# A pack's products ahead of the rest of its vector work, sums in two PSUM banks, one gate per pack for the gathers

## The chip, the core and the metric

The kernel runs on one core of a Trainium2 chip. The metric is the device time of one execution in microseconds (us). Engines are called by their names in the profile: PE (TensorE; PEld is its weight load), DVE (VectorE), ACT (ScalarE), POOL (GpSimd) and SP (SyncE, which only issues transfers here).

## The reference, cut to what matters

A graph of 12,500 nodes with 32 features and 400,000 edges, sorted by their target `dst`. Two layers, each in pre-norm form:

```python
h = jnp.maximum(_layernorm(x, axis=-1), 0.0)
x = x + _L0_gnn_ref(h, Wq, Wk, Wv, Wo, edge_index)      # attention over a node's edges
h = jnp.maximum(_layernorm(x, axis=-1), 0.0)
x = x + _L1_gnn_ref(h, edge_weight, edge_attr_3, edge_index, w1, b1, w2, b2)
```

The second layer is the tensor product, and the change lies in it:

```python
R = relu(abs_distances[:, None] @ w1 + b1) @ w2 + b2      # 384 radial weights an edge
Y = spherical_harmonics(rel_vec)
Fj = features[src]                                         # a gathered row of 32 an edge
# for each pair of blocks (lo, li) and each lf:
acc = acc + _NORM[i] * einsum('euv,ef,evi,ofi->euo', Rb[..., k], Yf, Fb, C)
out = zeros.at[dst].add(msg)                               # summed over a node's edges
```

## The kernel before

The program has five stages: a prologue (layer norm, projections), the attention over the edges (`attention`, its gathers at L534), the node update, the tensor product over the edges (`tensor_product`), and the node sums. In both edge stages the edges lie in 128 partitions by 3132 slots, and POOL gathers the source's row for each slot by one indirect DMA of 128 rows: 3132 of them for `kv` in the attention and 3132 for `feat` in the tensor product (L988).

The tensor product works in 58 chunks of 54 slots. A chunk is three packs of 18 slots, so there are 174 packs, and a turn of the loops has six (`TURN`). A pack is cut in six groups of three slots (`TRI`), called g0 to g5 here, and in two halves (`s` = 0 and 1) of three groups. For a pack:

- SP (`stack_up`) loads the hidden layer of the pack, transposed, into one of two slots of `stack` and `capped`.
- PE's `radial` multiplies it by `whigh` and `wlow`, six matmuls a group (L1003, L1004), into one of two places of `psR`. It runs two groups ahead of DVE: the place of group g is free when DVE's product of group g-2 is done.
- DVE's `products(i, j, s)` multiplies `psR` by the operands `ops`, three instructions a group (L1221), into `prod`. `fold` (L1230) adds a few of the 16 planes of `prod` in place.
- PE's `sums` adds the planes of `prod` for a half by matmuls against the identity into `psS` (L1014 for the planes that need no fold, L1017 for the folded ones). `psS` is one bank. ACT's `evict` (L1063) copies it to `red`.
- DVE's `rotate_back` (L1236), `add_back` (L1247, L1249, L1250) and `scan` (L1260) turn the previous pack's sums back, add them and scan them along the slots; ACT's `seeds` writes a part of `seed` and the flags `same_c` between, and `store` copies `run` out and issues its transfer.
- DVE's `rotate` (L1185) and `operands` (L1194) make the next pack's operands from the gathered `feat`; ACT's `scalars` and `turned` copy parts of `ops`.

The order is written out by hand on each engine. On DVE a pack goes: products of half 0, `rotate_back` of the pack before, `fold`, `add_back`, a signal `half_done`, products of half 1, `scan`, `fold`, `rotate` and `operands` of the next pack. On PE each half has its three radial groups (two ahead) and then its sums. POOL's 18 gathers of a pack go to one of three `feat` buffers, with two gates: the first nine wait for `feat_free` (raised in `operands`), the other nine for `half_done`. Both are primed with three.

```python
order = [j for j in range(FOLDS[s], JC) if not JC // 2 <= j < JC // 2 + FOLDS[s]]
```

`FOLDS` is 3 for half 0 and 2 for half 1, so the sums are 10 + 3 and 12 + 2 matmuls; the profile records two entries for each of these fp32 matmuls. `same_c` lies in PSUM, in the bank `psF`.

Of the kernel before, what the change touches and what calls it, by code (L numbers as in the profile page):

```python
# [31 lines left out]
ALU = mybir.AluOpType  # L32
ACT = mybir.ActivationFunctionType
AX = mybir.AxisListType

P = 128
# [15 lines left out]
GROUPS = 3  # L52
# [825 lines left out]
def tensor_product(nc, a, k):  # L878
# [11 lines left out]
    with ExitStack() as ctx:  # L890
# [23 lines left out]
        psR = pb("psR", [P, 2, TRI, 512])  # L914
        psS = pb("psS", [P, 512])
        psF = pb("psF", [P, 512])
        same_c = psF[:, 0:VU * P1].rearrange("p (c t) -> p c t", t=P1)

# [3 lines left out]
        feat_here = [sem(f"feat_here{h}") for h in range(PACKS)]  # L922
        feat_free, frame_free, stored = sem("feat_free"), sem("frame_free4"), sem("stored4")
# [4 lines left out]
        seeded, vec_done, chunk_begun, half_done = sem("seeded"), sem("vec_done4"), sem("chunk_begun4"), sem("half_done")  # L928

        with nc.Block(no_gpsimd_drain=True) as block:  # L930
# [44 lines left out]
            @block.gpsimd  # L975
            def _(pool):
                own_block(pool)
                with pool.Fori(0, PAIRS) as i:
                    for b in range(2):
                        pool.wait_ge(src_loaded[b], i * 16 + 16)  # L980
                        for h in range(PACKS):
                            pool.wait_ge(feat_free, i * TURN + b * PACKS + h + 1)
                            pool.sem_inc(chunk_begun, 1)
                            for t in range(PACK):
                                if t == MIDWAY:
                                    pool.wait_ge(half_done, i * TURN + b * PACKS + h + 1)
                                    pool.sem_inc(chunk_begun, 1)
                                nc.gpsimd.indirect_dma_start(  # L988
                                    feat[h][:, t, :], None, a["h2"],
                                    bass.IndirectOffsetOnAxis(ap=src_i[b][:, h * PACK + t:h * PACK + t + 1].bitcast(U32), axis=0)).then_inc(feat_here[h], 16)  # L990

            @block.tensor
            def _(pe):
                def radial(i, g):


                    pack, slot = g // GPP, g // GPP % 2
                    if g % GPP == 0:
                        pe.wait_ge(stacked[slot], (i + pack // 2) * 32 + 32)
                    pe.wait_ge(prod_done, 3 * (i * (2 * GPP) + g) + 3)  # L1000
                    for t in range(TRI):
                        at = ((g % GPP) * TRI + t) * P
                        nc.tensor.matmul(psR[:, g % 2, t, 0:384], stack[:, slot, at:at + P], whigh[:, :], start=True, stop=False)  # L1003
                        last_mm = nc.tensor.matmul(psR[:, g % 2, t, 0:384], capped[:, slot, at:at + P], wlow[:, :], start=False, stop=True)  # L1004
                    last_mm.then_inc(radial_ready, 1)

                def sums(i, s):

                    r, q = s % 2, i * (2 * SPP) + s
                    pe.wait_ge(sum_free, q + 2)  # L1010
                    pe.wait_ge(prod_done, q * (3 * GROUPS) + 3 * GROUPS + 6)
                    order = [j for j in range(FOLDS[s], JC) if not JC // 2 <= j < JC // 2 + FOLDS[s]]
                    for n, j in enumerate(order):
                        nc.tensor.matmul(psS[:, 0:GC].rearrange("p (t c) -> p t c", c=COLS), ident[:, :], prod[r][:, :, j, :], start=(n == 0), stop=False)  # L1014
                    pe.wait_ge(prod_ready, q + 1)
                    for j in range(FOLDS[s]):
                        last_mm = nc.tensor.matmul(psS[:, 0:GC].rearrange("p (t c) -> p t c", c=COLS), ident[:, :], prod[r][:, :, j, :], start=False, stop=(j == FOLDS[s] - 1))  # L1017
                    last_mm.then_inc(sum_ready, 1)


                pe.wait_ge(scales_steps, 1)
                nc.tensor.matmul(psS[0:1, 0:P], tops[:, :], ident[:, :], start=True, stop=True).then_inc(scales_back, 1)
                pe.wait_ge(scales_steps, 2)
                nc.tensor.matmul(psS[:, 0:3], ones_row[:, :], scales0[:, 1:4], start=True, stop=True).then_inc(scales_back, 1)
                pe.wait_ge(scales_steps, 3)
                radial(0, 0)
                radial(0, 1)

                def body(i, last):
                    for s in range(2 * SPP):  # L1030
                        for g in range(GROUPS * s + 2, GROUPS * s + GROUPS + 2):
                            if not last or g < 2 * GPP:
                                radial(i, g)
                        sums(i, s)
                for i in range(TWO_PACKS):
                    body(i, i == TWO_PACKS - 1)

            @block.scalar
            def _(act):
# [18 lines left out]
                def evict(i, j, s):  # L1058

                    if s == 0:  # L1060
                        act.wait_ge(red_free, i * TURN + j + 1)
                    act.wait_ge(sum_ready, i * (TURN * SPP) + j * SPP + s + 1)
                    nc.scalar.activation(red[j % 2][:, s * NINE:(s + 1) * NINE, :].rearrange("p t c -> p (t c)"),  # L1063
                                         psS[:, 0:GC], ACT.Copy, scale=scales[:, 2:3]).then_inc(sum_free, 1)

# [22 lines left out]
                def body(i, first, last):  # L1088
                    for j in range(TURN):
                        begun, more = not (first and j == 0), not (last and j == TURN - 1)  # L1090
                        if begun:
                            evict(i, j - 1, SPP - 1)
                            seeds(i, j - 1)
                        if not (first and j < 2):
                            store(i, j - 2)
                        for s in range(SPP - 1):
                            evict(i, j, s)
                        if more:
# [6 lines left out]
                pairs_apart(act, body)  # L1105
                evict(PAIRS - 1, TURN - 1, SPP - 1)
                seeds(PAIRS - 1, TURN - 1)
# [5 lines left out]
            def _(vec):  # L1113
                v = nc.vector
                for primed, n in ((feat_free, PACKS), (half_done, PACKS), (prod_done, 6), (sum_free, 2), (ops_free, 2),
                                  (red_free, 2), (scanned, 1), (run_copied, 1)):
                    vec.sem_inc(primed, n)
# [5 lines left out]
                step(v.memset(run[:, :, PACK:P1], 0.0))  # L1123
                step(v.memset(same_c, 0.0))
                vec.sem_inc(rows_set, 1)
# [23 lines left out]
                at0 = lambda n: tops0[:, n:n + 1]  # L1149
                step(v.tensor_reduce(at0(3), psS[0:1, 0:HID], axis=AX.X, op=ALU.max))  # L1150
                step(v.tensor_copy(at0(4), psS[0:1, HID:HID + 1]))
                step(v.tensor_tensor(at0(4), at0(4), at0(5), ALU.mult))
# [9 lines left out]
                vec.wait_ge(scales_back, 2)  # L1162
                step(v.tensor_copy(scales[:, 1:4], psS[:, 0:3]))
                step(v.tensor_scalar(new[:, 0, :], new[:, 0, :], scales[:, 1:2], None, ALU.mult))
# [24 lines left out]
                def operands(step, i, j):  # L1189

                    step.settle()
                    vec.wait_ge(ops_copied, i * TURN + j + 1)
                    vec.sem_inc(feat_free, 1)
                    add_up = lambda n: v.tensor_reduce(ops[j % 2][:, :, n * JC + VU:(n + 1) * JC], parts[:, :, n, :].rearrange("p t (i u) -> p t u i", i=3),  # L1194
# [9 lines left out]

                def products(i, j, s):

                    q = i * (TURN * SPP) + j * SPP + s
                    r = (j * SPP + s) % 2
                    vec.wait_ge(sum_free, q + 1)
                    if s == 0:  # L1210
                        vec.wait_ge(turned_ready, i * TURN + j + 1)
                    for third in range(GROUPS):
# [220 lines left out]
```

## Time and profile before

| | |
|---|---|
| median of 3 runs | 8775.19 us (8774.19 to 8779.57) |
| the profiled execution | span 10754.7 us; no other time is given for it |
| POOL busy | 6468.4 us (60%) |
| DVE busy | 5399.1 us (50%) |
| PE busy | 3832.9 us (36%), weight loads 2560.9 us |
| ACT busy | 1875.2 us (17%) |
| tensor product, 5107 to 10600 us of the span | PE busy 3761.22, DVE 3632.86, POOL 3059.14 us, mean granted clock 0.83 |

The profiled execution is 1979.5 us longer than the median of the timed runs. A share of busy time in the page is thus a share of a longer run, and a wait in the trace need not be in the timed runs. In a row, the first number is the start in us from the span's start, the second the duration; in brackets stands the engine's idle time before the instruction and what ended it.

### The profile page before, as it was taken

Reading aid. Unit: us, or ns where it says so; the run is one execution under the profiler, and the core shown is the slowest. Engines: PE = TensorE matmul, PEld = TensorE weight load, DVE = VectorE, ACT = ScalarE, POOL = GpSimd, SP = SyncE. Lnnn points to the kernel's source line nnn. Section 1 sums busy time; section 2 is a strip of 40 time slices with the busy share of each in tenths; the row PEclk is TensorE's granted clock in tenths of the full one; section 3 lists DMA queues with packets and bytes.
Section 4 is the critical chain, followed back from the end, with each engine's and each line's share of the span. In section 5 each row is a group of like instructions: output and inputs, shape, how many; then the busy total and the mean of one; then the engine's idle time right before and its main releaser. Section 6 shows DMA issues by size and latency. Waiting matters only on the chain. (4 is left out here: it accounts for less than half of the span.)

```text
span 10754.7 us, 65813 instructions
## 1 busy us (share of the span) xinstructions
PE 3832.9 (36%) x15884; PEld 2560.9 (24%) x15884; DVE 5399.1 (50%) x8641; ACT 1875.2 (17%) x2288; POOL 6468.4 (60%) x6677
## 2 busy tenths in 40 slices
PE   1000000000000000000576666666766666676663
PEld 0000000000000000000344444444444444444442
DVE  3223333333433333333566666666666666666664
ACT  0123222222222222221011111111111111111110
POOL 6776666666666666664555555555555555555554
PEclk6555555555555555555788888888888888888887
DMA  6334334334333433432122222222222222222221
GB/s 244 84 85 100 102 96 100 93 95 100 99 101 92 101 92 97 103 96 55 41 49 51 50 51 52 49 48 51 53 48 49 51 49 51 52 50 52 49 51 32
DMA packets 417113, 797.24 MB, mean 74 GB/s; under 512 B 166622, under 2 KB 244174, under 8 KB 404798
## 3 DMA queue, kind: packets, MB, share of 16 engines
q1 hardware_dynamic: 152488, 491.52, 16.4%
q0 software_dynamic: 213216, 166.16, 9.5%
q10 hardware_dynamic: 51126, 136.22, 3.3%
q8 instruction: 125, 2.05, 0.1%
q14 instruction: 158, 1.29, 0.0%
HBM read 499.75 MB, written 293.61 MB: 74 GB/s over the span
## 5 line engine op out<-in xcount | busy, mean ns | idle before, releaser
L988 POOL DMA_INDIRECT feat<-scratch_h,src x3132 | 3073.6, 981 | 2422.4 <-issue 1006.7
L534 POOL DMA_INDIRECT kv<-scratch_kv,src_i x3132 | 2992.4, 955 | 1533.4 <-issue 965.7
L1221 DVE TENSOR_TENSOR prod<-psR,ops 128x384 f32<-128x384 f32 (+1 forms) x3132 | 1936.3, 682 | 1807.0 <-remote 1335.6
L1014 PE MATMUL psS<-prod,ident 128*128 128x288 f32 x7656 | 2091.5, 433 | 2.1 <-DVE prod L1221 2.1
L1003 PE MATMUL psR<-whigh,stack 128*128 128x384 f16 x3132 | 1127.5, 361 | 1634.7 <-DVE prod L1221 1493.0
L1014 PEld LDWEIGHTS psS<-prod,ident 128*128 128x128 f32 x7656 | 1582.8, 208 | 470.5 <-issue 28.3
L798 PE MATMUL psA<-ident,tail 128*36 128x128 f32 x3 | 0.8, 414 | 4578.3 <-DVEq L823 4578.3
L1004 PE MATMUL psR<-wlow,capped 128*128 128x384 f16 x3132 | 1131.4, 362 | 96.7 <-issue 93.6
L798 PEld LDWEIGHTS psA<-ident,tail 128*36 128x36 f32 x3 | 0.3, 128 | 4578.5 <-DVEq L823 4578.4
L1003 PEld LDWEIGHTS psR<-whigh,stack 128*128 128x128 f16 x3132 | 323.8, 103 | 2081.8 <-DVE prod L1221 1693.0
L641 DVE TENSOR_TENSOR sq<-attr 128x162 f32<-128x162 f32 x58 | 19.1, 329 | 1518.4 <-DMA attr<-in_attr 1039.8
L1063 ACT ACTIVATE red<-psS,scales 128x288 f32<-128x288 f32 x348 | 174.5, 501 | 3418.8 <-remote 2177.7
L1017 PE MATMUL psS<-prod,ident 128*128 128x288 f32 x1740 | 480.5, 406 | 7.0 <-issue 7.0
L1004 PEld LDWEIGHTS psR<-wlow,capped 128*128 128x128 f16 x3132 | 327.2, 104 | 338.6 <-issue 180.8
L685 DVE TENSOR_TENSOR low<-psD,high 128x1728 f16<-128x1728 f32 x116 | 227.1, 1958 | 273.8 <-issue 160.2
L1017 PEld LDWEIGHTS psS<-prod,ident 128*128 128x128 f32 x1740 | 330.8, 190 | 98.6 <-issue 7.5
L572 ACT ACTIVATE psD<-w_row,b,w 128x1728 f32<-128x1728 f32 x116 | 208.2, 1794 | 776.3 <-issue 518.5
L1194 DVE TENSOR_REDUCE ops<-parts 128x144 f32<-128x432 f32 x522 | 306.0, 641 | 41.8 <-DVE parts L1185 22.5
L679 DVE TENSOR_TENSOR_SCAN psQ<-psQ,qseed 128x1760 f32<-128x1760 f32 x58 | 222.2, 3832 | 200.5 <-issue 200.2
L702 DVE TENSOR_TENSOR ev<-kv,psQ 128x1728 f32<-128x1728 f32 x58 | 178.1, 3071 | 277.5 <-ACT psQ L584 131.8
L1230 DVE TENSOR_TENSOR prod<-prod 128x864 f32<-128x864 f32 x348 | 310.1, 891 | 0.1
L1055 ACT ACTIVATE ops<-ops 128x144 f32<-128x144 f32 x174 | 56.1, 323 | 1436.7 <-DVE ops L1194 1212.6
(253 smaller groups left out, 4355.2 us busy)
## 6 DMA issues: line engine op xcount, KB each, us to landing
w_row<-in_wT SPq DMA_DIRECT2D x232, 432.0 KB
stack<-scratch_hid SPq DMA_DIRECT2D x174, 576.0 KB
scratch_state<-out ACTq DMA_DIRECT2D x58, 1080.0 KB
kv<-scratch_kv,src_i POOLq DMA_INDIRECT x3132
qin<-scratch_qexp SPq DMA_DIRECT2D x58, 864.0 KB
scratch_hid<-high SPq DMA_DIRECT2D x232, 216.0 KB
scratch_hid<-low SPq DMA_DIRECT2D x232, 216.0 KB
feat<-scratch_h,src POOLq DMA_INDIRECT x3132
```

What stands on the lines that cost most here:

```text
L534: nc.gpsimd.indirect_dma_start(kv[b][:, t, :], None, a["kv"], bass.IndirectOffsetOnAxis(ap=src_i[b][:, t:t + 1].bitcast(U32), axis=0)).the ...
L572: nc.scalar.activation(units, w_row[q][:, :], ACT.Relu, bias=b1[:, :], scale=w1[:, :]).then_inc(units_ready, 1)
L679: step(v.tensor_tensor_scan(flat(qrun), flat(qrun), flat(qseed), 0.0, ALU.mult, ALU.add))
L685: v.tensor_tensor(low[q][:, :], units, high[q][:, :], ALU.subtract).then_inc(split_done, 1)
L988: nc.gpsimd.indirect_dma_start(feat[h][:, t, :], None, a["h2"], bass.IndirectOffsetOnAxis(ap=src_i[b][:, h * PACK + t:h * PACK + t + 1].bi ...
L1003: nc.tensor.matmul(psR[:, g % 2, t, 0:384], stack[:, slot, at:at + P], whigh[:, :], start=True, stop=False)
L1004: last_mm = nc.tensor.matmul(psR[:, g % 2, t, 0:384], capped[:, slot, at:at + P], wlow[:, :], start=False, stop=True)
L1014: nc.tensor.matmul(psS[:, 0:GC].rearrange("p (t c) -> p t c", c=COLS), ident[:, :], prod[r][:, :, j, :], start=(n == 0), stop=False)
L1017: last_mm = nc.tensor.matmul(psS[:, 0:GC].rearrange("p (t c) -> p t c", c=COLS), ident[:, :], prod[r][:, :, j, :], start=False, stop=(j == ...
L1194: add_up = lambda n: v.tensor_reduce(ops[j % 2][:, :, n * JC + VU:(n + 1) * JC], parts[:, :, n, :].rearrange("p t (i u) -> p t u i", i=3), ...
L1221: v.tensor_tensor(to[:, :, :, lo:lo + n], psR[:, g % 2, :, frm:frm + n * JC].rearrange("p t (j u) -> p t j u", j=JC), ops[j % 2][:, ts, x ...
L1230: v.tensor_tensor(prod[r][:, :, 0:FOLDS[s], :], prod[r][:, :, 0:FOLDS[s], :], prod[r][:, :, JC // 2:JC // 2 + FOLDS[s], :], ALU.add).then_ ...
```

## The change

In the tensor product alone:

- DVE's order in a pack becomes: products of half 0, `fold`, products of half 1, `fold`, then `rotate_back`, `add_back` and `scan` of the pack before, then `rotate` and `operands` of the next.
- `products` no longer waits for ACT's evictions (`sum_free`), but for PE's sums of the pack before (`sum_ready`, q - 1), which have read the same `prod` buffer.
- `psS` has two banks, one for each half; PE's sums of a half wait for the eviction of the same half of the pack before, not for the last eviction.
- PE takes the radial groups in another rhythm: g2 to g5 of a pack, sums of half 0, then the first two groups of the next pack, sums of half 1.
- ACT evicts both halves of a pack one behind the other, at the head of the next pack's turn.
- POOL has one gate a pack, `turn_begun`, which DVE raises behind the products of g0; `feat_free` and `half_done` are gone.
- `same_c` moves from PSUM to SBUF; the bank goes to `psS`.

```diff
-        psS = pb("psS", [P, 512])
-        psF = pb("psF", [P, 512])
-        same_c = psF[:, 0:VU * P1].rearrange("p (c t) -> p c t", t=P1)
+        psS = pb("psS", [P, SPP, 512])
+        same_c = sb("same_c4", [P, VU, P1])
@@ POOL
-                            pool.wait_ge(feat_free, i * TURN + b * PACKS + h + 1)
-                            pool.sem_inc(chunk_begun, 1)
+                            pool.wait_ge(turn_begun, i * TURN + b * PACKS + h + 1)
+                            pool.sem_inc(pack_begun, 1)
                             for t in range(PACK):
-                                if t == MIDWAY:
-                                    pool.wait_ge(half_done, i * TURN + b * PACKS + h + 1)
-                                    pool.sem_inc(chunk_begun, 1)
@@ PE, sums
-                    pe.wait_ge(sum_free, q + 2)
+                    into = psS[:, s % SPP, 0:GC].rearrange("p (t c) -> p t c", c=COLS)
+                    pe.wait_ge(sum_free, q + 1)
@@ PE, body
-                        for g in range(GROUPS * s + 2, GROUPS * s + GROUPS + 2):
+                        ahead = (2, GPP) if s % SPP == 0 else (GPP, GPP + 2)
+                        for g in range(s // SPP * GPP + ahead[0], s // SPP * GPP + ahead[1]):
@@ ACT, body
-                            evict(i, j - 1, SPP - 1)
+                            for s in range(SPP):
+                                evict(i, j - 1, s)
                             seeds(i, j - 1)
                         if not (first and j < 2):
                             store(i, j - 2)
-                        for s in range(SPP - 1):
-                            evict(i, j, s)
@@ DVE, operands
-                    vec.sem_inc(feat_free, 1)
@@ DVE, products
-                    vec.wait_ge(sum_free, q + 1)
+                    if not (first and j == 0):
+                        vec.wait_ge(sum_ready, q - 1)
...
+                        if g == 0:
+                            vec.sem_inc(turn_begun, 1)
@@ DVE, body
-                        products(i, j, 0)
+                        products(i, j, 0, first)
+                        fold(i, j, 0)
+                        products(i, j, 1, first)
+                        fold(i, j, 1)
                         if begun:
                             rotate_back(step, i, j - 1)
-                        fold(i, j, 0)
-                        if begun:
                             add_back(step, i, j - 1)
-                        vec.sem_inc(half_done, 1)
-                        products(i, j, 1)
-                        if begun:
                             scan(step, i, j - 1)
-                        fold(i, j, 1)
                         if more:
                             rotate(step, i, j + 1)
                             operands(step, i, j + 1)
```

## Rows read from the trace of the kernel before

**Rows 1.** The page: span and costliest groups (busy, mean ns, idle before, releaser).

```profile
span 10754.7 us, 65813 instructions
...
L988 POOL DMA_INDIRECT feat<-scratch_h,src x3132 | 3073.6, 981 | 2422.4 <-issue 1006.7
L534 POOL DMA_INDIRECT kv<-scratch_kv,src_i x3132 | 2992.4, 955 | 1533.4 <-issue 965.7
L1221 DVE TENSOR_TENSOR prod<-psR,ops 128x384 f32<-128x384 f32 (+1 forms) x3132 | 1936.3, 682 | 1807.0 <-remote 1335.6
```

**Rows 2.** Timeline, DVE and POOL around one long wait of DVE.

```profile
7502.88 1.05 DVE L1230 TENSOR_TENSOR prod<-prod 128x864 f32<-128x864 f32 x1
7503.05 1.70 POOL L988 DMA_INDIRECT feat<-scratch_h,src  x1 [0.30 <-issue]
...
7518.78 1.89 DVE L1221 TENSOR_TENSOR prod<-psR,ops 128x768 f32<-128x768 f32 x3 [9.31 <-remote]
...
7525.27 0.95 POOL L988 DMA_INDIRECT feat<-scratch_h,src  x1 [8.56 <-DVEq L1193]
```

**Rows 3.** Timeline, a gather that starts during a scan.

```profile
8527.89 1.55 DVE L1260 TENSOR_TENSOR_SCAN run<-psF,seed 128x152 f32<-128x152 f32 x4
8528.04 0.95 POOL L988 DMA_INDIRECT feat<-scratch_h,src  x1 [0.31 <-issue]
```

**Rows 4.** Timeline of DVE, one pack from its operands to the next.

```profile
8531.89 1.76 DVE L1194 TENSOR_REDUCE ops<-parts 128x144 f32<-128x432 f32 x3 [0.24 <-issue]
8533.85 5.47 DVE L1221 TENSOR_TENSOR prod<-psR,ops 128x768 f32<-128x768 f32 x9 [0.20 <-DVE ops L1194]
8539.24 1.63 DVE L1236 TENSOR_TENSOR back<-red,frame 128x432 f32<-128x432 f32 x3
8540.79 1.05 DVE L1230 TENSOR_TENSOR prod<-prod 128x864 f32<-128x864 f32 x1
...
8543.70 3.67 DVE L1221 TENSOR_TENSOR prod<-psR,ops 128x768 f32<-128x768 f32 x6
8558.33 1.88 DVE L1221 TENSOR_TENSOR prod<-psR,ops 128x768 f32<-128x768 f32 x3 [10.96 <-remote]
...
8561.61 0.73 DVE L1230 TENSOR_TENSOR prod<-prod 128x576 f32<-128x576 f32 x1
...
8564.14 1.76 DVE L1194 TENSOR_REDUCE ops<-parts 128x144 f32<-128x432 f32 x3 [0.24 <-DVE parts L1185]
```

**Rows 5.** Timeline of DVE in the last pack, after POOL's last gather.

```profile
10594.22 3.66 DVE L1221 TENSOR_TENSOR prod<-psR,ops 128x768 f32<-128x768 f32 x6
10598.34 1.89 DVE L1221 TENSOR_TENSOR prod<-psR,ops 128x768 f32<-128x768 f32 x3 [0.46 <-PE psR L1004]
...
10607.97 1.64 DVE L1236 TENSOR_TENSOR back<-red,frame 128x432 f32<-128x432 f32 x3 [5.62 <-ACT red L1063]
10609.87 0.20 DVE L1247 COPY seed<-run 128x32 f32<-128x32 f32 x1 [0.26 <-DVE back L1236]
```

**Rows 6.** Timeline of DVE in the first pack, a fold behind its product.

```profile
5131.43 1.89 DVE L1221 TENSOR_TENSOR prod<-psR,ops 128x768 f32<-128x768 f32 x3 [11.68 <-remote]
5133.35 1.06 DVE L1230 TENSOR_TENSOR prod<-prod 128x864 f32<-128x864 f32 x1
```

**Rows 7.** Timeline of PE: sums and radial groups, and sums at a low clock.

```profile
8516.90 6.72 PE L1014 MATMUL psS<-prod,ident 128*128 128x288 f32 x20
...
8529.01 5.98 PE L1014 MATMUL psS<-prod,ident 128*128 128x288 f32 x24
...
8535.80 0.33 PE L1003 MATMUL psR<-whigh,stack 128*128 128x384 f16 x1
...
8539.38 0.34 PE L1003 MATMUL psR<-whigh,stack 128*128 128x384 f16 x1 [0.64 <-DVE prod L1221]
...
8540.36 5.01 PE L1014 MATMUL psS<-prod,ident 128*128 128x288 f32 x20
...
8546.67 0.33 PE L1003 MATMUL psR<-whigh,stack 128*128 128x384 f16 x1
```

More of the change, by code:

```diff
@@ L922, in tensor_product @@
         feat_here = [sem(f"feat_here{h}") for h in range(PACKS)]
-        feat_free, frame_free, stored = sem("feat_free"), sem("frame_free4"), sem("stored4")
+        turn_begun, frame_free, stored = sem("turn_begun"), sem("frame_free4"), sem("stored4")
         radial_ready, prod_done, prod_ready, sum_ready, sum_free = (sem(n) for n in (
@@ L927, in tensor_product @@
             "ops_copied", "turned_ready", "turned_copied", "ops_free", "flags_ready4", "red_free", "scanned", "run_copied"))
-        seeded, vec_done, chunk_begun, half_done = sem("seeded"), sem("vec_done4"), sem("chunk_begun4"), sem("half_done")
+        seeded, vec_done, pack_begun = sem("seeded"), sem("vec_done4"), sem("pack_begun")
         with nc.Block(no_gpsimd_drain=True) as block:
@@ L1013, in sums @@
                     for n, j in enumerate(order):
-                        nc.tensor.matmul(psS[:, 0:GC].rearrange("p (t c) -> p t c", c=COLS), ident[:, :], prod[r][:, :, j, :], start=(n == 0), stop=False)
+                        nc.tensor.matmul(into, ident[:, :], prod[r][:, :, j, :], start=(n == 0), stop=False)
                     pe.wait_ge(prod_ready, q + 1)
                     for j in range(FOLDS[s]):
-                        last_mm = nc.tensor.matmul(psS[:, 0:GC].rearrange("p (t c) -> p t c", c=COLS), ident[:, :], prod[r][:, :, j, :], start=False, stop=(j == FOLDS[s] - 1))
+                        last_mm = nc.tensor.matmul(into, ident[:, :], prod[r][:, :, j, :], start=False, stop=(j == FOLDS[s] - 1))
                     last_mm.then_inc(sum_ready, 1)
                 pe.wait_ge(scales_steps, 1)
-                nc.tensor.matmul(psS[0:1, 0:P], tops[:, :], ident[:, :], start=True, stop=True).then_inc(scales_back, 1)
+                nc.tensor.matmul(psS[0:1, 0, 0:P], tops[:, :], ident[:, :], start=True, stop=True).then_inc(scales_back, 1)
                 pe.wait_ge(scales_steps, 2)
-                nc.tensor.matmul(psS[:, 0:3], ones_row[:, :], scales0[:, 1:4], start=True, stop=True).then_inc(scales_back, 1)
+                nc.tensor.matmul(psS[:, 0, 0:3], ones_row[:, :], scales0[:, 1:4], start=True, stop=True).then_inc(scales_back, 1)
                 pe.wait_ge(scales_steps, 3)
@@ L1063, in evict @@
                     nc.scalar.activation(red[j % 2][:, s * NINE:(s + 1) * NINE, :].rearrange("p t c -> p (t c)"),
-                                         psS[:, 0:GC], ACT.Copy, scale=scales[:, 2:3]).then_inc(sum_free, 1)
+                                         psS[:, s, 0:GC], ACT.Copy, scale=scales[:, 2:3]).then_inc(sum_free, 1)
                 def seeds(i, j):
@@ L1105, in _ @@
                 pairs_apart(act, body)
-                evict(PAIRS - 1, TURN - 1, SPP - 1)
+                for s in range(SPP):
+                    evict(PAIRS - 1, TURN - 1, s)
                 seeds(PAIRS - 1, TURN - 1)
@@ L1114, in _ @@
                 v = nc.vector
-                for primed, n in ((feat_free, PACKS), (half_done, PACKS), (prod_done, 6), (sum_free, 2), (ops_free, 2),
+                for primed, n in ((turn_begun, PACKS), (prod_done, 6), (sum_free, 2), (ops_free, 2),
                                   (red_free, 2), (scanned, 1), (run_copied, 1)):
@@ L1123, in _ @@
                 step(v.memset(run[:, :, PACK:P1], 0.0))
-                step(v.memset(same_c, 0.0))
+                step(v.memset(same_c[:, :, :], 0.0))
                 vec.sem_inc(rows_set, 1)
@@ L1149, in _ @@
                 at0 = lambda n: tops0[:, n:n + 1]
-                step(v.tensor_reduce(at0(3), psS[0:1, 0:HID], axis=AX.X, op=ALU.max))
-                step(v.tensor_copy(at0(4), psS[0:1, HID:HID + 1]))
+                step(v.tensor_reduce(at0(3), psS[0:1, 0, 0:HID], axis=AX.X, op=ALU.max))
+                step(v.tensor_copy(at0(4), psS[0:1, 0, HID:HID + 1]))
                 step(v.tensor_tensor(at0(4), at0(4), at0(5), ALU.mult))
@@ L1162, in _ @@
                 vec.wait_ge(scales_back, 2)
-                step(v.tensor_copy(scales[:, 1:4], psS[:, 0:3]))
+                step(v.tensor_copy(scales[:, 1:4], psS[:, 0, 0:3]))
                 step(v.tensor_scalar(new[:, 0, :], new[:, 0, :], scales[:, 1:2], None, ALU.mult))
@@ L1203, in frame_of, with products @@
                     return frame[j // PACKS % 2][:, at:at + PACK, n * 3:(n + 1) * 3]
-                def products(i, j, s):
+                def products(i, j, s, first):
                     q = i * (TURN * SPP) + j * SPP + s
                     r = (j * SPP + s) % 2
-                    vec.wait_ge(sum_free, q + 1)
+                    if not (first and j == 0):
+                        vec.wait_ge(sum_ready, q - 1)
                     if s == 0:
```

## The prediction

> **What bounds the kernel now.** I read the page first. The profiled execution's span is 10754.7 us [rows 1] and the median of the timed runs 8775.19 us, so 1979.5 us of the trace are not in what is timed. Before any row can be priced, that excess has to be placed. The groups of POOL give the place. POOL's gathers of the tensor product take 3073.6 us and have 2422.4 us of idle time before them, of which 1006.7 us are issue time (0.30 us between two gathers, all along) [rows 1, 3]; the other 1415.7 us are waits for a gate. For the attention's gathers it is 1533.4 - 965.7 = 567.7 us [rows 1]. Together POOL waits 1983.4 us. The span less these waits is 8771.3 us, 4 us from the median. I read this as: in the timed runs POOL hardly waits in either edge stage, and gathers at 0.95 + 0.30 us apiece set the pace of both.
>
> Then the timeline, for what makes POOL wait in the trace. DVE has one long wait a pack, shown as remote, 9 to 11 us, before products whose matmuls PE's records show as long done [rows 2, 4]; they make up 1335.6 us of that group's 1807.0 us of idle time [rows 1]. The wait at 7518.78 ends two microseconds after POOL's last gather ended (7525.27 less the 8.56 us of idle is 7516.71) [rows 2], so engines are held while gathers run and let go when POOL pauses. Were that in the timed runs too, the stage would last as long there as in the trace, and the 1979.5 us would have no source. I take it for a trait of the profiled execution.
>
> Priced so, the stage before is: POOL (3073.6 + 1006.7) / 174 = 23.45 us a pack. For DVE I add start to start over a pack, without the long wait [rows 4, 5]: g0 to g3 8543.70 - 8533.85 = 9.85; g3 to g5 10598.34 - 10594.22 = 4.12, in which 0.46 us is a true wait for PE, seen after POOL's last gather; g5 to `operands` 8564.14 - 8558.33 = 5.81; `operands` to the next g0 8533.85 - 8531.89 = 1.96. The sum is 21.74 us. DVE thus has 1.7 us a pack to spare against POOL's 23.45, or 300 us in the stage.
>
> **The change, part by part.** All sums are differences against the profiled execution cleared of its waits, 8771.3 us, which stands for the 8775.19 us median.
>
> *DVE's order.* The same instructions run, none is added. What differs is which stand behind their own input. Before, `rotate_back` starts 0.08 us ahead of its predecessor's end (8539.24 against 8533.85 + 5.47 = 8539.32) [rows 4]; a fold straight behind its product starts 0.03 us after the end (5133.35 against 5131.43 + 1.89 = 5133.32) [rows 6]. That is 0.11 us more for each of two folds, and I take the same for `scan` straight behind `add_back`: 0.33 us. `back` to the next instruction is 1.55 us when a fold stands between (8540.79 - 8539.24) [rows 4], and 1.90 us when the copy waits for it (10609.87 - 10607.97) [rows 5]: 0.35 us. Given back is the wait at g5, 0.46 us and its lost overlap of 0.08, since PE's radial group 5 now comes ahead of the sums. Net 0.33 + 0.35 - 0.54 = +0.14 us: DVE's pack is 21.9 us. Hidden behind POOL's 23.45; without that cover it costs 0.14 x 174 = 24 us.
>
> *PE's order and the two banks.* A radial group takes 0.98 us (8539.38 to 8540.36), the sums of half 0 take 6.31 (8540.36 to 8546.67), those of half 1 6.79 (8529.01 to 8535.80) [rows 7]. Before, PE has two short loops with DVE in a pack; after, one long one: g3 ends, radial 5, sums 0, two radials, sums 1, radial 2 of the next pack, in all 0.98 + 6.31 + 1.96 + 6.79 + 0.98 = 17.02 us with some 0.3 of handovers, and then DVE's g2, fold and g3, 1.82 + 0.03 + 0.97 + 1.82 = 4.6 us [rows 4]. The loop is 22.0 us, under 23.45 by 1.5 us. It costs nothing at full clock. The second bank takes away PE's wait for the last eviction, which here was long satisfied: nothing. The new wait of `products` for `sum_ready` has all of DVE queued behind it; sums 0 of the pack before end some 6 us ahead of it and sums 1 some 4 us. `rotate_back` comes at 12.6 us of a pack, while sums 1 of the pack before end at about 2.5 us and both evictions follow: ACT's later eviction is covered too. SP's loads of `stack` are released earlier or as before. No transfer is added or resized.
>
> *The gates.* `turn_begun` replaces `feat_free`, raised 3.8 us later (`operands` to the end of g0: 1.96 + 1.82) [rows 4], and `half_done` goes. Behind the wait stand 18 gathers, and behind them DVE's `rotate` and ACT's `scalars`. With three buffers both old gates belong to an iteration that ended two packs before, when POOL is the late one, and so does the new one: nothing. If DVE were the late one, 18 x 1.25 = 22.5 us of gathers would still not fit into 21.9 us of DVE, so POOL falls back to being late.
>
> *`same_c` in SBUF.* This is the one part that touches the pacing engine. A gather that starts under a fold (two inputs in SBUF) takes 1.70 in place of 0.95 us [rows 2]; one that starts under the scan, which now reads PSUM and SBUF, takes its 0.95 us [rows 3]. After the change the scan has two SBUF inputs. The mean gather is 0.981 us [rows 1], 0.031 above the undisturbed, 0.56 us a pack, for some 7.1 us of such DVE work (`rotate_back` 1.63, fold and adds 2.91, second fold and `rotate` 2.53) [rows 4]. The scan's 1.55 us in proportion gives 0.12 us a pack, 21 us in all. Bounds: nothing, as in rows 3; and 0.75 us a pack, what the fold took from one gather, 131 us. I take the proportion, since `rotate_back`, like the scan, is a string of short instructions.
>
> The Trainium skill ("SBUF — State Buffer", Who interferes with whom) says that a DVE instruction with two SBUF inputs excludes a GpSimd instruction that reads SBUF, and one with at most one such input does not. By that rule the trace agrees in both rows; it speaks against this part of the change.
>
> Sum: 0 + 0 + 0 + 21, on 8775.19 about 8796 us.
>
> **The rivals.**
>
> *The scan holds the gathers as the fold does.* If the four scans in a row keep a gather out until the last of them, each pack pays up to the 0.75 us of rows 2, 8775 + 131 = 8906 us. For it: the fold's row. Against it: the mean stretch of 0.031 us with four such stretches of DVE work in each pack. By the rule of the Trainium skill just named each scan instruction excludes the gather by itself; rows of the string of three in `rotate_back` would tell, and I hold this case at 0.1.
>
> *PE's long loop.* It has 1.5 us to spare only at full clock. At the low clock the first 20 entries of sums 0 take 6.72 in place of 5.01 us [rows 7]. If PE drops once a pack, the loop grows by two such pieces, to over 25 us; once in three packs it costs about 0.5 us a pack, 8775 + 90 = 8865 us. In the trace the drops follow pauses of PE of 7 us and more, which the timed runs should not have. Decides if PE idles long enough in each pack. 0.15.
>
> *DVE sets the pace.* If the timed gathers are cheaper than 1.21 us apiece, 21.74 us of DVE rules before and 21.9 after: 8775 + 24 = 8799 us. Against it is the 4 us agreement above. 0.1. The number is that of my forecast, for another reason.
>
> *Faster.* The gate in the middle of a pack costs POOL something in the timed runs after all, or the folds now fall where fewer gathers start. Of the 0.56 us of stretch and of a gate's wait a half a microsecond at most can go: 0.28 us a pack is 8775 - 49 = 8726 us. It decides where the mean gather falls below 0.965 us or POOL's ninth gather had ended before `half_done`. For it: the pauses at the gates in the trace, 1415.7 us; against it: that they vanish in the sum above. 0.2.
>
> **How the numbers follow.** The forecast, POOL sets the pace and only the scan's share is paid, has 0.45: 8796 us, its own range 8765 to 8840. About 0.2% (17.5 us) is what a measurement of this kernel can tell from no change; the forecast's 21 us lie on that edge. From the forecast's 0.45 I give 0.2 to no change, 0.2 to slower, 0.05 to faster; of the faster case 0.17 to faster and 0.03 to none; DVE's case is split 0.03 and 0.07; the other two are slower. That makes 0.22, 0.26 and 0.52, and I move a little from slower to the others for mechanisms that I do not see: 0.26, 0.28, 0.46. The range reaches from the faster rival's further end, 8700, to the scan's upper bound, 8910.
>
> **What would show it.** In the trace after: the gathers' busy time a little above 3073.6 us, with stretched gathers under the scan; span less POOL's gate waits again near the timed median; in DVE's rows `fold` 0.03 us behind its product and copy 0.26 us behind `back`; no wait of g5 for radial 5, and a wait of g2 of about nothing. The span itself may move by hundreds of microseconds either way, because the long waits hang on when POOL pauses, and that says nothing of the timed run. The prediction is wrong if the timed runs do have those long waits, in part: then the single gate, which lets 18 gathers run without a pause, or the new order, moves the time by far more than 0.14 or 0.12 us a pack.

## The result and the profile after

The changed kernel takes 8661.47 us (median of 4, 8657.69 to 8667.72) where the kernel before takes 8774.69 us (8758.42 to 8779.57) on the same chip: a ratio of 0.9874, 95% interval 0.986 to 0.9888. That is 113 us less, where 21 us more were forecast.

Two sorts of chips have to be kept apart to read what follows. The eighteen runs fell on five chips. On two of them the kernel before takes a median of 8776 us, within 10 us in every execution. On the other three its medians are 10,572 to 10,801 us, and no execution came under 10,547; the trace shown ahead of the prediction (span 10754.7 us) [rows 1] looks like those. I call them the quick and the held chips. That the chip decides is inferred from which runs fell where. One held chip was met twice, twelve minutes apart, with medians of 10,801 and 10,572 us, so how much is lost is not fixed by the chip. The verdict above is one of a quick chip, so the profile to set beside the one after is that of the kernel before on a quick chip, which the fifth run gave (8768.16 us).

The page of the kernel before on the quick chip, in its form of [rows 1]:

```profile
span 8766.3 us, 65813 instructions
...
L988 POOL DMA_INDIRECT feat<-scratch_h,src x3132 | 3238.5, 1034 | 974.6 <-issue 952.9
L534 POOL DMA_INDIRECT kv<-scratch_kv,src_i x3132 | 2963.8, 946 | 959.5 <-issue 959.5
L1221 DVE TENSOR_TENSOR prod<-psR,ops 128x384 f32<-128x384 f32 (+1 forms) x3132 | 1922.2, 683 | 201.0 <-PE psR L1004 129.3
```

The page of the changed kernel:

```profile
span 8655.9 us, 65313 instructions
...
L984 POOL DMA_INDIRECT feat<-scratch_h,src x3132 | 3129.9, 999 | 974.4 <-issue 954.0
L534 POOL DMA_INDIRECT kv<-scratch_kv,src_i x3132 | 2964.7, 947 | 959.1 <-issue 959.1
L1219 DVE TENSOR_TENSOR prod<-psR,ops 128x384 f32<-128x384 f32 (+1 forms) x3132 | 1914.6, 680 | 120.0 <-PE psR L1000 46.5
```

Read the two L98x lines against each other. POOL's idle time before the gathers is 974.6 and 974.4 us, nearly all of it issue: in neither kernel does POOL wait for a gate. So POOL sets the pace in both, at (3238.5 + 974.6) / 174 = 24.21 us a pack before and (3129.9 + 974.4) / 174 = 23.59 after. The busy time of the gathers fell by 108.6 us, of the 110.4 us between the two spans. The mean gather went from 1.034 to 0.999 us, and nothing else is needed to account for the gain. On the fifth run's own chip the changed kernel's trace (the sixth run) says the same: 3137.1 us of gathers, 101.4 less, with a span 104.1 us shorter.

Which gathers are long? The timeline of the kernel before on the quick chip (start, duration, what; only rows of DVE and POOL):

```profile
6004.55 1.06 DVE L1230 TENSOR_TENSOR prod<-prod 128x864 f32<-128x864 f32 x1
6005.24 1.18 POOL L988 DMA_INDIRECT feat<-scratch_h,src  x1 [0.30 <-issue]
6005.52 0.20 DVE L1247 COPY seed<-run 128x32 f32<-128x32 f32 x1
6005.61 0.95 DVE L1249 TENSOR_TENSOR seed<-back 128x432 f32<-128x432 f32 x1
6006.60 0.95 DVE L1250 TENSOR_TENSOR seed<-seed,back 128x432 f32<-128x432 f32 x1
6006.73 1.64 POOL L988 DMA_INDIRECT feat<-scratch_h,src  x1 [0.31 <-issue]
...
6013.41 1.56 DVE L1260 TENSOR_TENSOR_SCAN run<-psF,seed 128x152 f32<-128x152 f32 x4
6013.67 0.94 POOL L988 DMA_INDIRECT feat<-scratch_h,src  x1 [0.31 <-issue]
```

And of the changed kernel:

```profile
6011.52 1.64 DVE L1236 TENSOR_TENSOR back<-red,frame 128x432 f32<-128x432 f32 x3
6012.72 1.25 POOL L984 DMA_INDIRECT feat<-scratch_h,src  x1 [0.30 <-issue]
6013.39 0.20 DVE L1247 COPY seed<-run 128x32 f32<-128x32 f32 x1 [0.23 <-DVE back L1236]
6013.49 0.95 DVE L1249 TENSOR_TENSOR seed<-back 128x432 f32<-128x432 f32 x1
6014.28 0.99 POOL L984 DMA_INDIRECT feat<-scratch_h,src  x1 [0.30 <-issue]
6014.48 0.95 DVE L1250 TENSOR_TENSOR seed<-seed,back 128x432 f32<-128x432 f32 x1
6015.46 1.57 DVE L1260 TENSOR_TENSOR_SCAN run<-same_c,seed 128x152 f32<-128x152 f32 x4
6015.57 1.11 POOL L984 DMA_INDIRECT feat<-scratch_h,src  x1 [0.30 <-issue]
```

A gather that starts inside a DVE instruction with two inputs in SBUF ends 0.82 us after that instruction does, as if it had begun just before its end: 6006.73 + 1.64 = 6008.37 is 0.82 after 6006.60 + 0.95. In the kernel before one held gather leads to the next: released by the fold, the next start falls at the head of the second addition, and that gather takes 1.64 us. In the changed kernel the short pieces of `rotate_back` come first, the following start falls near the end of the first addition, and that gather takes 0.99. It is held by the one instruction that it starts in, not by a row of them: `rotate_back` is three instructions of 0.6 us, 1.64 us together, and no gather that starts under it takes over 1.39 us.

I counted all 3132 gathers of each timeline by the DVE instruction that had begun last when they start, if it was still running; the excess is over 0.945 us:

| starts under | before: gathers, mean us, excess us | after: gathers, mean us, excess us |
|---|---|---|
| fold | 234, 1.330, 90 | 146, 1.122, 26 |
| the two additions | 172, 1.645, 120 | 172, 1.030, 15 |
| `rotate_back` | 175, 1.129, 32 | 207, 1.177, 48 |
| `rotate` | 177, 1.165, 39 | 194, 1.261, 61 |
| scan (flags in PSUM, then SBUF) | 180, 0.944, 0 | 302, 1.019, 22 |
| reduction of `operands` (one input) | 218, 0.944, 0 | 189, 0.944, 0 |
| products (one input in PSUM) | 1452, 0.944, -2 | 1541, 0.944, -2 |
| no DVE instruction | 513, 0.944, -1 | 370, 0.944, 0 |

The eleven others of each start under the stage's setup. Fold and additions gave back 169 us; `rotate_back`, `rotate` and the scan took 60. The difference, 109 us, is the gain. The other three quick traces of these two orders have nearly the same means: 1.038 us in the kernel before without its gate in the middle, 1.002 in the changed kernel and in the changed kernel with such a gate.

### The profile page after: what moved, and what is told of

Same layout as the page of the kernel before. It is cut to its first block and busy times, and to the rows that moved or that the text cites. A ratio compares the mean times of both kernels' runs of the same rounds, so it can differ in the third digit from the quotient of the medians.

```text
span 8655.9 us, 65313 instructions
## 1 busy us (share of the span) xinstructions
PE 3580.7 (41%) x15884; PEld 2443.4 (28%) x15884; DVE 5469.7 (63%) x8641; ACT 1869.0 (22%) x2288; POOL 6499.0 (75%) x6677
## 5 line engine op out<-in xcount | busy, mean ns | idle before, releaser
L984 POOL DMA_INDIRECT feat<-scratch_h,src x3132 | 3129.9, 999 | 974.4 <-issue 954.0
L1011 PE MATMUL psS<-prod,ident 128*128 128x288 f32 x7656 | 1965.6, 414 | 0.0
L1011 PEld LDWEIGHTS psS<-prod,ident 128*128 128x128 f32 x7656 | 1489.2, 196 | 413.1 <-issue 11.0
L999 PE MATMUL psR<-whigh,stack 128*128 128x384 f16 x3132 | 1069.3, 342 | 581.3 <-DVE prod L1219 571.0
L688 DVE TENSOR_TENSOR qk<-psQ,kv 128x1728 f32<-128x1728 f32 x58 | 113.5, 1957 | 1559.1 <-DMA kv<-scratch_kv,src_i 1559.1
L1000 PE MATMUL psR<-wlow,capped 128*128 128x384 f16 x3132 | 1067.3, 341 | 0.0
L1047 ACT ACTIVATE ops<-feat 128x144 f32<-128x144 f32 x174 | 56.2, 323 | 2644.0 <-DMA feat<-scratch_h,src 2644.0
L1014 PE MATMUL psS<-prod,ident 128*128 128x288 f32 x1740 | 478.8, 406 | 0.0
L1183 DVE TENSOR_TENSOR parts<-feat,frame 128x432 f32<-128x432 f32 x522 | 286.6, 603 | 172.3 <-DMA feat<-scratch_h,src 172.3
L1014 PEld LDWEIGHTS psS<-prod,ident 128*128 128x128 f32 x1740 | 330.6, 190 | 91.3
L587 ACT ACTIVATE out<-sums 128x1944 f32<-128x1944 f32 x58 | 220.2, 3796 | 466.4 <-DVEq L707 466.4
L1236 DVE TENSOR_TENSOR back<-red,frame 128x432 f32<-128x432 f32 x522 | 287.1, 604 | 5.1 <-ACT red L1061 5.1
```

Of the source, the lines that this page charges most:

```text
L984: nc.gpsimd.indirect_dma_start(feat[h][:, t, :], None, a["h2"], bass.IndirectOffsetOnAxis(ap=src_i[b][:, h * PACK + t:h * PACK + t + 1].bi ...
L1011: nc.tensor.matmul(into, ident[:, :], prod[r][:, :, j, :], start=(n == 0), stop=False)
L1014: last_mm = nc.tensor.matmul(into, ident[:, :], prod[r][:, :, j, :], start=False, stop=(j == FOLDS[s] - 1))
L1183: step(v.tensor_tensor(parts[:, :, n, :].rearrange("p t (i u) -> p t i u", i=3), f[:, :, VU:D].rearrange("p t (i u) -> p t i u", i=3), fra ...
L1236: step(v.tensor_tensor(back[:, :, n, :].rearrange("p t (o u) -> p t o u", o=3), red[j % 2][:, :, (n + 1) * VU:(n + 2) * VU].rearrange("p t ...
```

## The experiments

**The kernel before, profiled again.** No edit. On a held chip:

> The kernel before, unchanged, profiled again, because the profile shown with it lasted 10754.7 us and the one of the changed kernel only 8655.9 us. Theory A (DVE is late in the undisturbed kernel before, so POOL waits at its gates, the one in the middle above all): POOL's gathers of the tensor product wait on DVE for about 110 us in total (0.6 us a pack), their mean stays at 0.98 to 1.0 us. Theory B (POOL never waits, what changed is how DVE's two-input work stretches the gathers): no gate waits, and the gathers' busy time is about 110 us above the 3129.9 us of the changed kernel, a mean of 1.03 us. Both: a span near 8773 us if the execution is not held up as the first one was.

10584.83 us, beside timed executions of 10,548 to 10,600 us on the same chip, so the first trace was no accident of one profiled execution. On a quick chip:

> The kernel before once more, to get a profile of an execution near 8775 us. On the chip of the first four runs even timed executions of it took 10575 us, with the long waits in them: these waits are real there, not a trait of profiling. Expected 8775 us on a chip like that of the comparison, 10575 us on one like the last. Where it is 8775: Theory A, POOL waits at its gates for some 110 us; Theory B, no gate waits and gathers of 1.03 us.

8768.16 us. POOL's waits for a gate come to 1.2 us in all, and the mean gather is 1.034 us: Theory B.

**The changed kernel again**, on the quick chip:

> The changed kernel, to have it beside the parts on one chip. 8661 us where before is 8775. Where before is 10575: the single gate alone would give +190 us as it did before, the order alone with a mid gate gave -184 us; if they add, about 10580 us, no change.

8658.69 us against 8775.79, ratio 0.9865 (0.9848 to 0.9881), mean gather 1.002 us.

**The gate in the middle of a pack.** Taken out of the kernel before:

```diff
-                                if t == MIDWAY:
-                                    pool.wait_ge(half_done, i * TURN + b * PACKS + h + 1)
-                                    pool.sem_inc(chunk_begun, 1)
...
-                        vec.sem_inc(half_done, 1)
```

On the held chip:

> The kernel before without the gate in the middle of a pack (half_done); all else as before. Theory A: the gate was the cost, so about 8665 us, as the changed kernel. Theory B: the gate never held POOL, 8775 us within 15.

10762.3 us, ratio 1.0188 (1.0163 to 1.0214): slower, which neither theory had. On the quick chip:

> The kernel before without the gate in the middle of a pack. Where before is 8775: Theory A says 8665 us, Theory B says 8775 us within 15. Where before is 10575: 10762 us as measured.

8777.03 us, ratio 1.0003 (0.9993 to 1.0012): nothing, as Theory B said. Put into the changed kernel:

```diff
+                                if t == MIDWAY:
+                                    pool.wait_ge(half_done, i * TURN + b * PACKS + h + 1)
...
+                        if g == GROUPS:
+                            vec.sem_inc(half_done, 1)
```

On the held chip:

> The changed kernel with a gate in the middle of a pack put back (raised by DVE behind the products of g3, at about 8.3 us of a pack; before it was raised at 9.9 us). Theory A (gates hold POOL): most of the gain is gone, 8740 to 8775 us. Theory B, or a gain that comes from the order on DVE: 8661 us within 15.

10390.24 us, ratio 0.9834 (0.9809 to 0.9858). On the quick chip:

> The changed kernel with a gate in the middle of a pack. Where before is 8775: Theory A says 8740 to 8775 us, Theory B 8661 us within 15. Where before is 10575: 10390 us as measured.

8664.15 us, ratio 0.9874 (0.9858 to 0.989): the whole gain, with the gate. Theory A is out: on a quick chip the gates are no part of it.

**The flags in SBUF**, in the kernel before, on the held chip:

```diff
-        same_c = psF[:, 0:VU * P1].rearrange("p (c t) -> p c t", t=P1)
+        same_c = sb("same_c4", [P, VU, P1])
```

> The kernel before with the flags same_c in SBUF instead of PSUM; all else as before. The prediction's step: the scan now keeps gathers out, +21 us (0 to 131), 8796 us. Theory B would allow another sign, since a gather that is held moves the later ones: 8760 to 8796 us. Theory A: the gate absorbs it, 8775 us within 15.

10573.33 us, ratio 1.0 (0.9988 to 1.0011). POOL has time to spare there, so the time says nothing of a quick chip; the trace does. Of the gathers that start under the scan, the 146 of the first run had a mean of 0.943 us and none took over 1; here 126 have a mean of 1.041, and 70 of them took over 1. Nothing but the place of the flags differs between the two kernels.

**DVE's order alone, and all but DVE's order.** The two halves of the change's core:

```diff
                         products(i, j, 0)
-                        if begun:
-                            rotate_back(step, i, j - 1)
                         fold(i, j, 0)
-                        if begun:
-                            add_back(step, i, j - 1)
                         vec.sem_inc(half_done, 1)
                         products(i, j, 1)
-                        if begun:
-                            scan(step, i, j - 1)
                         fold(i, j, 1)
+                        if begun:
+                            rotate_back(step, i, j - 1)
+                            add_back(step, i, j - 1)
+                            scan(step, i, j - 1)
```

The other kernel is the changed one with the lines of the old DVE order back. On a held chip:

> The kernel before with DVE's new order alone (products, fold, products, fold, then the previous pack's work); PE's and ACT's order, one sums bank, both gates (the middle one raised behind the first fold) and the flags in PSUM as before. Theory B (POOL's gathers set the pace and are stretched by DVE's two-input work according to where it falls): the order is what counts, mean gather near 1.00 us, 8640 to 8690 us where before is 8775. Rival C (the gain comes from PE's order, by which SP's loads of stack start earlier and no longer meet a pack's last gathers): 8775 us within 15.

> The changed kernel with DVE's old order put back; PE's and ACT's order, two banks, one gate and flags in SBUF as in the changed kernel. Theory B: mean gather near 1.03 us or a little more for the flags, 8760 to 8800 us where before is 8775. Rival C: about 8661 us.

11598.16 us against 10800.68, ratio 1.0732 (1.0709 to 1.0755), and 10394.43 us, ratio 0.9637 (0.9595 to 0.9679). On a quick chip:

> As the ninth run, hoped for on a chip where before takes 8775 us. Theory B: mean gather near 1.00 us, 8640 to 8690 us, also without the second bank and PE's order, as long as DVE's waits for PE stay under POOL's 23.5 us a pack. Rival C (PE's order and the earlier loads of stack): 8775 us within 15. Where before is held up (10600 to 10800 us): 7% slower, as measured.

> As the tenth run. Where before is 8775: Theory B 8760 to 8800 us with a mean gather of 1.03 us, Rival C about 8661 us. Where before is held up: 3.6% faster, as measured.

9307.63 us, ratio 1.0605 (1.0588 to 1.0623), and 9320.42 us, ratio 1.0621 (1.0603 to 1.0639), against 8775.55 us. Both theories missed. The page of the first:

```profile
L988 POOL DMA_INDIRECT feat<-scratch_h,src x3132 | 3097.8, 989 | 1604.9 <-issue 863.4
L1221 DVE TENSOR_TENSOR prod<-psR,ops 128x384 f32<-128x384 f32 (+1 forms) x3132 | 1934.3, 681 | 921.0 <-PE psR L1004 848.1
```

and of the second:

```profile
L984 POOL DMA_INDIRECT feat<-scratch_h,src x3132 | 3341.7, 1067 | 1364.9 <-issue 908.3
L1219 DVE TENSOR_TENSOR prod<-psR,ops 128x384 f32<-128x384 f32 (+1 forms) x3132 | 1934.4, 681 | 1072.7 <-PE psR L1000 1072.4
```

DVE waits 848.1 and 1072.4 us for radial groups, and POOL now waits for DVE: the pace has passed to the loop of PE and DVE. In the timeline of the first, the wait sits at g5, whose radial group stands behind the sums:

```profile
6011.41 5.01 PE L1014 MATMUL psS<-prod,ident 128*128 128x288 f32 x20
6016.27 1.62 PE L1017 MATMUL psS<-prod,ident 128*128 128x288 f32 x6
6017.72 0.33 PE L1003 MATMUL psR<-whigh,stack 128*128 128x384 f16 x1
...
6018.90 1.89 DVE L1221 TENSOR_TENSOR prod<-psR,ops 128x768 f32<-128x768 f32 x3 [4.68 <-PE psR L1004]
```

With the old PE order DVE's moved work no longer lies over PE's sums, and 4.68 us show. In the second the wait sits at g2 instead, with a median of 5.06 us. The two orders belong together: these two kernels cost 532 and 545 us against the kernel before, the pair keeps DVE under POOL's pace. A part of that is TensorE's clock. From 4400 to 8400 us the mean granted clock is 0.87 in both traces, against 0.96 in the kernel before and 0.97 in the changed one: it falls to the lower of its two levels once in nearly every pack. PE's busy time is 298 us above that of the kernel before in the first and 176 us above that of the changed kernel in the second. How much of the 532 and 545 us this makes is not separated.

The gathers' means, 0.989 and 1.067, follow DVE's order and not PE's, and in the second kernel SP's loads of `stack` go out some 6 us before a pack's last gather ends, without any gain in them, which speaks against Rival C. But with POOL waiting the means are no measure of what the pair does.

**A pause at the head of a pack**, one memset of 128x384 ahead of `products(i, j, 0)`, in the changed kernel and in the kernel before:

> The changed kernel with one more DVE instruction at the head of each pack, a memset of 128x384 that nothing reads (about 0.38 us, 66 us over 174 packs if DVE set the pace). Theory B: DVE has over 1 us a pack to spare, so the 66 us do not show as such, but all of DVE's later work is moved by 0.38 us against the gathers, and the time moves by up to 50 us either way with the mean gather. A rival by which DVE's length counts: 8661 + 66 = 8727 us.

> The kernel before with the same extra memset at the head of each pack. Theory B: the stretched gathers shift, so the time moves by up to 100 us either way, faster as likely as not, though DVE does more; the mean gather tells. A rival by which DVE's length counts: 8775 + 66 = 8841 us.

They fell on a held chip: 10751.75 us against 10800.68, ratio 0.9964 (0.9933 to 0.9994), and 10771.78 us, ratio 0.9965 (0.9953 to 0.9978). Inconclusive for a quick chip, where they were not run, so the most direct test of Theory B, the same work of DVE at another moment, is missing.

**One reduction for the two additions:**

```diff
-                    step(v.tensor_tensor(seed[:, VU:D, 1:P1], turn(0), turn(1), ALU.add))
-                    step(v.tensor_tensor(seed[:, VU:D, 1:P1], seed[:, VU:D, 1:P1], turn(2), ALU.add), hold=False)
+                    step(v.tensor_reduce(seed[:, VU:D, 1:P1], back[:, :, :, :].rearrange("p t n x -> p x t n"),
+                                         axis=AX.X, op=ALU.add), hold=False)
```

> The kernel before, with the two additions of add_back (two inputs in SBUF each) replaced by one reduction over the three turned parts (one input); order, gates, banks and flags as before. Of the kernel before's 279 us of stretched gathers (mean 1.034 against 0.945 undisturbed, times 3132), 119 us lie with gathers that overlap the second addition or both. Theory B (two-input work on DVE stretches POOL's gathers, and these set the pace): mean gather near 0.995 us, 8775 - 120 = 8655 us, 8620 to 8700. Rival D (the stretch comes from DVE's work whatever its inputs, or from the DMA traffic): 8775 us within 15. Where before is held up (over 10500 us) the run says little.

> The changed kernel with the same replacement. There some 45 us of the stretch lie with gathers that overlap the additions. Theory B: 8661 - 40 = 8620 us, 8580 to 8661, with a mean gather near 0.985 us. Rival D: 8661 us within 15.

> As the fifteenth run, hoped for where before takes 8775 us. Theory B: mean gather near 0.995 us and 8655 us, 8620 to 8700. Rival D: 8775 us within 15. Where before is held up: 2.6% slower, as measured.

> As the sixteenth run. Where before is 8775: Theory B 8620 us, 8580 to 8661, mean gather near 0.985 us; Rival D 8661 us within 15. Where before is held up: 0.6% slower than before, as measured.

Both pairs fell on held chips: in the kernel before 10845.25 us, ratio 1.0265 (1.0248 to 1.0282), and 10896.29, 1.0115 (1.0088 to 1.0142); in the changed one 10627.55, 1.006 (1.0028 to 1.0092), and 10838.89, 1.0066 (1.0041 to 1.0091). Their times neither bear out nor refute Theory B. The edit had a flaw besides: the reduction takes 3.34 us where the two additions take 1.9. What it shows is in the trace of the seventeenth run:

```profile
6939.33 3.35 DVE L1248 TENSOR_REDUCE seed<-back 128x432 f32<-128x1296 f32 x1
6940.44 0.95 POOL L988 DMA_INDIRECT feat<-scratch_h,src  x1 [0.30 <-issue]
6941.69 0.94 POOL L988 DMA_INDIRECT feat<-scratch_h,src  x1 [0.30 <-issue]
```

Two gathers start under one long instruction with a single SBUF input, and neither is held. Of the 410 that start under this reduction not one takes over 1 us; of the 93 under the second addition in the kernel before on the quick chip every one does. So Rival D, a stretch by any work of DVE, is out by the trace, though not by the times.

No experiment beat the changed kernel on a quick chip; with the gate in the middle it is as quick. On held chips two of its versions beat the kernel before by more than 1%: this one by 1.7%, and the one with DVE's old order by 3.6%, the very kernel that loses 6.2% on a quick chip.

## Why the prediction was wrong

*What bounds the kernel* was right for the quick chips: POOL, which waits nowhere, in both kernels. The sum of 8771.3 us met the quick trace's span of 8766.3, and that was luck in part. The quick trace has 165 us more of busy time in the tensor product's gathers (3238.5 against 3073.6), and 170 us less of everything else in that sum. So the agreement within 4 us, on which I built, was no sign that the gathers were priced rightly. The 9 us waits are no trait of profiling either: the timed executions on a held chip are as long as the trace. And in the held trace POOL paused during a good part of DVE's two-input work, so its mean of 0.981 us [rows 1] hid most of the stretching: on a quick chip, where POOL does not wait, it is 1.034, an excess of 1.6 us a pack where I worked with 0.56.

*The step that failed* is the first part, DVE's order: "Hidden behind POOL's 23.45". DVE's length was hidden, as said: its busy time grew by 61 us (5408.8 to 5469.7) and POOL did not wait for it. Its order was not, because it sets which gathers start under which instruction. I priced this contention for the one instruction that changed its inputs and took all the rest as unmoved, at nothing. It fell from 281 us to 150 without the scan, about 130 us that the sum lacks, and turned 21 us more into 113 us less. My rival for it ("the folds now fall where fewer gathers start") had the mechanism and a net 0.28 us a pack; it was 0.62. The sign I had named, a busy time of the gathers a little above 3073.6 us, came true (3129.9) and misled, since the number to compare with is 3238.5.

*`same_c` in SBUF:* forecast 21 us; the gathers under the scan have an excess of 22 us. The size is right, by some luck: the same proportion, taken of the quick kernel's 1.6 us a pack, would have given 61 us. The rival by which the four scans together keep a gather out is refuted: the longest under a scan takes 1.13 us, so each instruction holds it by itself.

*DVE's handovers:* copy 0.23 us behind `back` (6013.39), as forecast; before, nearly every pack waits at g5 for PE, with a median of 0.46 us, as forecast; after, of 165 packs 37 wait at g2 and 62 at g5, nearly all under 0.5 us, and all idle time before the products is 120.0 us against 201.0. Right in kind, hidden.

*PE's long loop:* it fits under POOL's pace, as forecast, and the low clock was no rival: 0.97 in the stage, which is near the upper level. That it fits only with both orders changed I had not asked. My reading that the clock drops follow pauses of PE of 7 us and more does not hold in the trace I took it from. Around 8507 us the matmuls L1004 already take 0.48 us in place of 0.33, ahead of a pause of 6.63 us; and the quick traces, where PE has no such pauses, have 82 drops before and 75 after, nearly all of 3.4 us.

*The gates:* nothing, as forecast, for a quick chip. The last sentence of the prediction named the case of the held chips, where a gate is worth 1.9%.

What is shown: POOL sets the pace, the gathers' busy time is the gain, and within the packs only gathers that start under two-input DVE instructions are held: in all twenty timelines none that starts under another, or under none, takes over 1 us. (Outside the packs there is one exception: the gather that starts under the setup's cast into `whigh`, with one input, takes 1.09 us.) What is argued from the timelines alone: that the new sequence shortens the chain of held gathers. A kernel with the same DVE work at other moments on a quick chip would test it; mine fell on held chips. How much of the changed phase comes from DVE's order and how much from the earlier landing below is open, and with it which part of the change is to be thanked.

## What to carry to other kernels

When one engine does nothing but issue gathers and sets the pace, ask of each instruction on DVE not how long it is but how many SBUF inputs it has and what starts beside it: a gather is held to the end of the one two-input instruction that it starts in, so long ones (0.95 us here) cost it up to 0.7 us, shorter ones (0.45 to 0.6 us) up to 0.2 to 0.45, and an instruction with one input in PSUM nothing. Check that the profiled execution is of the same sort as the timed ones before pricing anything from it; a span 23% above the median is a reason to take the trace again. Two hand-written orders on engines that feed each other have to be moved together: each half here costs 6% without the other.

## What the runs showed of the hardware that I had not expected

*Held chips.* On three chips of five DVE waits, in every kernel run there, while gathers run, and goes on when POOL pauses [rows 2]. The kernel before has 144 such waits of over 4 us, shown as remote, in its first trace, and at the median they end 2.4 us after a gather did, where 0.3 us is the usual distance to the next gather; the seven traces of quick chips have none. The same program takes 8775 or 10,570 to 10,800 us. The order counts for more there: without the gate in the middle 1.9% is lost, by DVE's order alone 7.3%, and all but DVE's order gains 3.6%. Why, and what holds the engines, no run shows. The changed kernel itself was not run on a held chip.

*A gather is held by one instruction at a time.* In the quick traces a held gather ends 0.81 to 0.84 us after the instruction of its start, 0.75 after a scan. So under the four short scans (0.45 us each) it loses at most 0.19 us and 0.07 in the mean, under an addition of 0.95 us as much as 0.7. The Trainium skill ("SBUF — State Buffer", Who interferes with whom) has the rule by number of SBUF inputs, and the counts above agree with it for every instruction of the packs, two inputs (1.02 to 1.65 us in the mean) and at most one (0.94).

*When a pack's last gather lands.* In the kernel before `rotate` starts some 4 us after the last gather of its pack ended. SP's loads of `stack` and `capped` go out just ahead of that gather, and that they delay it is argued from the times alone:

```profile
6011.74 0.34 SPq L948 DMA_DIRECT2D stack<-scratch_hid  x1
6012.18 0.47 SPq L949 DMA_DIRECT2D capped<-scratch_hid  x1
6012.42 0.94 POOL L988 DMA_INDIRECT feat<-scratch_h,src  x1 [0.30 <-issue]
...
6017.52 1.65 DVE L1185 TENSOR_TENSOR parts<-feat,frame 128x432 f32<-128x432 f32 x3 [1.90 <-DMA feat<-scratch_h,src]
```

In the changed kernel the load is issued at 6009.09, the last gather ends at 6015.57 + 1.11 = 6016.68 and `rotate` starts 1.4 us later, at 6018.10. The median over the stage is 4.1 us before and 1.5 after. The load of `capped` lands 5.4 us after its issue at the median, which from 6012.18 is 6017.6, when `rotate` starts. POOL does not wait for it, so it costs nothing here by itself.
